# A megakernel of attention and a mixed feed-forward block: the gate's product, the last residuals and the order of PSUM banks

## The reference

```python
x = x + attn(_layernorm(x), Wqkv, bqkv, Wo, bo)
x = x + ffn(_layernorm(x), gate_w, up_w, down_w, fc1_w, fc2_w, expert_w, ln_gamma, ln_beta)

# attn: qkv = x @ Wqkv + bqkv (D = 256); softmax(q k^T / 16) v; @ Wo + bo
# ffn:
logits = x @ gate_w                                   # 1024 -> 8
routing_weights, _ = top_k(logits, 2)
shared_out = relu(x @ up_w) ** 2 @ down_w             # 1024 -> 2048 -> 1024
moe_out = (x @ fc1_w) @ expert_w * sum(routing_weights)   # 1024 -> 512 -> 512
routed_out = moe_out @ fc2_w                          # 512 -> 1024
ffn = _layernorm(shared_out + routed_out) * ln_gamma + ln_beta
```

## Time and profile before

| | |
|---|---|
| median of three runs | 2235.44 us (2233.91 to 2235.86) |
| profiled execution, its own time | 2224.65 us |
| profiled execution, span (first to last instruction) | 2222.9 us |
| PE busy | 2194.1 us (99%), 14963 matmuls |
| DVE busy | 1481.5 us (67%) |
| ACT busy | 623.9 us (28%) |
| POOL busy | 631.7 us (28%) |
| granted TensorE clock | 0.999 of full speed |
| HBM traffic | 202 GB/s over the span |

### The profile page before, as it was taken

How to read it: one execution, slowest core, us unless ns; L and a number is a source line. 1 busy time by engine, 2 the same in 40 slices (tenths; PEclk the granted TensorE clock), 3 DMA queues, 4 the chain that set the end, 5 groups by cost and what they waited for, 6 DMA issues and landing times.

```text
span 2222.9 us, 36661 instructions
## 1 busy us (share of the span) xinstructions
PE 2194.1 (99%) x14963; PEld 1418.4 (64%) x14963; DVE 1481.5 (67%) x1846; ACT 623.9 (28%) x966; POOL 631.7 (28%) x526
## 2 busy tenths in 40 slices
PE   7999999999999999999999999999999999999998
PEld 6756556666665444685487478468558748846853
DVE  7767387788985899776666377366556637737624
ACT  4334244345322664232022012112202201211210
POOL 2322000000002779255145024214404403421411
PEclk9999999999999999999999999999999999999999
DMA  9898288999897888879877987986997798798775
GB/s 234 196 215 220 58 183 234 243 242 224 185 212 203 291 310 287 283 238 286 272 215 225 278 273 220 287 283 205 279 273 231 225 284 259 220 295 264 205 231 167
DMA packets 527705, 530.05 MB, mean 238 GB/s; under 512 B 334896, under 2 KB 355504, under 8 KB 527536
## 3 DMA queue, kind: packets, MB, share of 16 engines
q1 hardware_dynamic: 513760, 495.70, 78.7%
q10 hardware_dynamic: 12912, 28.85, 4.2%
q0 software_dynamic: 864, 3.15, 0.4%
HBM read 375.03 MB, written 73.41 MB: 202 GB/s over the span
## 4 chain that ended last, share of the span: by engine, by line
PE 93%; DVE 4%; issue 2%; POOL 1%; DMA 0%; ACT 0%; DVEq 0%; ACTq 0%; POOLq 0%; SPq 0%
PE psum L99 62%; PE psum L2326 27%; PE psum L2270 4%; POOL arena L329 1%; DVE arena L2017 0%; PE psum L2235 0%; DVE arena L990 0%; DVE arena L540 0%; DVE c_ystats L2011 0%; PE psum L2236 0%; DMA arena<-arena 0%; DVE b_mx L1007 0%; DVE arena L2027 0%; DVE a_stats L496 0%; DVE arena L2029 0%
## 5 line engine op out<-in xcount | busy, mean ns | idle before, releaser
L99 PE MATMUL psum<-arena 128*128 128x256 f16 (+1 forms) x10920 | 1461.2, 297 | 5.0 <-ACT arena L879 1.5
L99 PEld LDWEIGHTS psum<-arena 128*128 128x128 f16 x10920 | 1067.5, 98 | 395.9 <-issue 4.5
L2326 PE MATMUL psum<-arena 128*128 128x512 f16 x2856 | 617.7, 379 | 0.0
L2326 PEld LDWEIGHTS psum<-arena 128*128 128x128 f16 x2856 | 279.4, 98 | 335.5
L1672 POOL TENSOR_TENSOR arena<-arena 128x256 f32<-128x256 f32 x70 | 98.4, 1405 | 350.6 <-ACT arena L1833 350.6
L879 ACT ACTIVATE arena<-psum,b_nb,consts 128x512 f32<-128x512 f32 x128 | 97.9, 774 | 196.3 <-DVE b_nb L1011 196.3
L1659 POOL TENSOR_TENSOR arena<-arena 128x256 f32<-128x256 f32 x68 | 50.5, 743 | 333.5 <-DVE arena L2113 277.0
L1990 DVE TENSOR_TENSOR arena<-arena 128x1536 f16<-128x1536 f32 (+1 forms) x28 | 60.6, 2165 | 121.5 <-ACT arena L1732 121.1
L1810 ACT ACTIVATE arena<-arena 128x768 f16<-128x768 f32 x68 | 57.3, 843 | 270.6 <-DVE arena L2113 229.5
L1814 ACT ACTIVATE arena<-arena 128x1024 f16<-128x1024 f32 x68 | 71.9, 1057 | 210.7 <-POOL arena L1665 207.7
L2073 DVE TENSOR_TENSOR arena<-arena 128x768 f16<-128x768 f32 x68 | 89.1, 1310 | 41.1 <-ACT arena L1810 40.9
(11 more groups left out here) (179 smaller groups left out, 1847.8 us busy)
## 6 DMA issues: line engine op xcount, KB each, us to landing
arena<-ws_out SPq DMA_DIRECT2D x238, 512.0 KB, 4.8
arena<-ws_in SPq DMA_DIRECT2D x210, 512.0 KB, 4.6
arena<-in_attn_x SPq DMA_DIRECT2D x64, 512.0 KB, 4.9
arena<-x SPq DMA_DIRECT2D x64, 512.0 KB, 6.6
arena<-ws_in SPq DMA_DIRECT2D x70, 256.0 KB, 4.8
x<-arena SPq DMA_DIRECT2D x32, 512.0 KB, 3.5
out<-arena SPq DMA_DIRECT2D x31, 512.0 KB, 6.2
ws_in<-arena SPq DMA_DIRECT2D x30, 512.0 KB, 4.5
```

The lines of the kernel that those rows point to most:

```text
L99: last = nc.tensor.matmul(out, lhs(a, c), rhs(b, c), start=(c == 0 and n == 0), stop=(c == chunks - 1 and n == len(PRODUCTS) - 1))
L2326: mm = nc.tensor.matmul(product_banks(m)[:, u, :], rS[c][:, a, LEFT[m], u * P:(u + 1) * P], w2[slot_of(i, d_slot(i, m, q))][:, cc, b, :], ...
```

## The change

Four edits, with what goes with them:

1. The gate of blocks 1 to 7. G11 is common to both halves of the block. It now has two rows of its own in `pG` (`G_ROWS` is 6: two with Y1 and G22, two with G21, two with G11), and DVE adds it to both halves with one more instruction, which waits for the first. A gate has 32 chunk products of two matmuls instead of 40. Block 0's gate keeps its four rows on PE; on DVE its sum of high and low is now two instructions of two tiles each. `g16` and `lg` grow from four to six rows, and for space the raw gate weights are scaled in place.
2. In the last block POOL adds beta to the residual of all four tiles, and DVE takes L2024 for all four.
3. In merged blocks (2 to 7) the statistics of the half of a tile that the outstanding product does not touch are taken before the wait for that product (`early_stats`).
4. The eight banks of the routed products begin with bank 7 instead of bank 6. The waits are changed to match: a routed product waits for one more of ACT's copies in block 0 and for the counts of its bank in block 1, the gate for one `rt_added` instead of two, and step p = 0 of the next block for five instead of six.

```diff
-BANKS_F, BANKS_U, BANK_G, BANKS_R = (7, 0), (0, 1, 2, 3), 7, (6, 7, 0, 1, 2, 3, 4, 5)
+BANKS_F, BANKS_U, BANK_G, BANKS_R = (7, 0), (0, 1, 2, 3), 7, (7, 0, 1, 2, 3, 4, 5, 6)
...
-    gs = sb("gs", [P, KC, NE], F32)
+    gs = graw
...
+    G_ROWS = 3 * HT
+    gate_rows = lambda i: TILES if first_turn(i) else G_ROWS
...
-            for q in range(R_EARLY, TILES):
+            for q in range(TILES):
                 pool.wait_ge(xres_in[q % 2], 16 * (2 * i + q // 2 + 1))
                 pool.tensor_tensor(xres[q % 2], xres[q % 2], beta, ALU.add).then_inc(xres_summed, 1)
...
-            nc.scalar.activation(g16[:], pG, ACT.Copy).then_inc(g_free, 1)
+            n = gate_rows(i)
+            nc.scalar.activation(g16[:, 0:n], pG[:, 0:n], ACT.Copy).then_inc(g_free, 1)
...
-        steps.done(dve.tensor_tensor(lg[:], g16[:, :, 0:NE], g16[:, :, NE:2 * NE], ALU.add))
+        if first_turn(i):
+            for t in range(0, TILES, HT):
+                at = slice(t, t + HT)
+                steps.done(dve.tensor_tensor(lg[:, at], g16[:, at, 0:NE], g16[:, at, NE:2 * NE], ALU.add))
+        else:
+            steps.link(dve.tensor_tensor(lg[:], g16[:, :, 0:NE], g16[:, :, NE:2 * NE], ALU.add))
+            halves = lg[:, 0:TILES].rearrange("p (h u) e -> p h u e", h=2)
+            shared = lg[:, TILES:].rearrange("p (h u) e -> p h u e", h=1).to_broadcast([P, 2, HT, NE])
+            steps.done(dve.tensor_tensor(halves, halves, shared, ALU.add))
...
-                if last and q >= R_EARLY:
+                if last:
-                    dve.wait_ge(xres_summed, q - R_EARLY + 1)
+                    dve.wait_ge(xres_summed, q + 1)
...
+        def early_stats(i, last, q, h):
+            steps.at(start + i * PER_BLOCK + ROUTE + (-q if last else NORM_S * TILES) + OUT * q)
+            steps.done(dve.bn_stats(ystats[:, h, :], acc[:, r_order(i)[q], h * BANK:(h + 1) * BANK]))
...
                     for u in range(HT):
-                        n = HT * (m - M3) + u
+                        n, h = HT * (m - M3) + u, m - M3
+                        early_stats(i, last, n, 1 - h)
...
-                        routed(i, last, range(n, n + 1))
+                        routed(i, last, range(n, n + 1), halves=(h,), done=1)
...
-                pe.wait_ge(rt_added, R_TILES * i + 2)
+                pe.wait_ge(rt_added, R_TILES * i + 1)
...
-            parts = ((Y1, 0), (G11, 0), (G22, KH)) if t < HT else ((G11, 0), (G21, KH))
+            parts = (((Y1, 0), (G22, KH)), ((G21, KH),), ((G11, 0),))[kind]
...
-        for t in range(TILES):
+        for t in range(gate_rows(i)):
...
-                    pe.wait_ge(acc_copied, n + 1)
+                    pe.wait_ge(acc_copied, min(n + 2, R_TILES))
-                    pe.wait_ge(d_added, added_by(i) + (3, 5, 6, 7)[n // 2])
+                    pe.wait_ge(d_added, added_by(i) + (5, 6, 7, 3)[BANKS_R[n] // HALVES])
...
-                        pe.wait_ge(rt_added, R_TILES * i + (6, R_TILES)[p])
+                        pe.wait_ge(rt_added, R_TILES * i + (5, R_TILES)[p])
```

More of the change, by code:

```diff
@@ L1195, in mixture @@
     beta = place(AT["c_beta"], [H], F32)
-    g16 = sb("g16", [P, TILES, 2 * NE], F32)
-    lg = sb("lg", [P, TILES, NE], F32)
+    G_ROWS = 3 * HT
+    g16 = sb("g16", [P, G_ROWS, 2 * NE], F32)
+    lg = sb("lg", [P, G_ROWS, NE], F32)
     top = sb("top", [P, TILES, 8], F32)
@@ L1217, in mixture @@
     u_half = lambda p, q: u_bank(p, q).rearrange("p (c n) -> p c n", c=2)
-    pG = bank(BANK_G)[:, 0:TILES * 2 * NE].rearrange("p (t e) -> p t e", t=TILES)
+    pG = bank(BANK_G)[:, 0:G_ROWS * 2 * NE].rearrange("p (t e) -> p t e", t=G_ROWS)
+    gate_rows = lambda i: TILES if first_turn(i) else G_ROWS
     e_in, c2_in, gb_in = sem("e_in"), sem("c2_in"), sem("gb_in")
@@ L1888, in act_program @@
         turns(body)
-    NORM, NORM_S, ROUTE, OUT = 4, 3, 1 + TILES + 1, 5
+    NORM, NORM_S, ROUTE, OUT = 4, 3, 2 + TILES + 1, 5
     BEFORE = 2
@@ L1995, in routing, with routed @@
             assert steps.n == ROUTE
-        def routed(i, last, tiles=range(TILES)):
-            steps.at(start + i * PER_BLOCK + ROUTE + (-max(tiles[0] - R_EARLY, 0) if last else NORM_S * TILES) + OUT * tiles[0])
+        def routed(i, last, tiles=range(TILES), halves=(), done=0):
+            steps.at(start + i * PER_BLOCK + ROUTE + (-tiles[0] if last else NORM_S * TILES) + OUT * tiles[0] + done)
             for q in tiles:
                 t = r_order(i)[q]
-                for h in range(HALVES):
+                for h in halves or range(HALVES):
                     n = HALVES * q + h
@@ L2029, in routed @@
                 dve.tensor_tensor(row, row, xres[q % 2], ALU.add).then_inc(out_ready, 1)
-            assert steps.n == OUT * len(tiles) - len([q for q in tiles if last and q >= R_EARLY])
+            assert steps.n == OUT * len(tiles) - done - (len(tiles) if last else 0)
+        def early_stats(i, last, q, h):
+            steps.at(start + i * PER_BLOCK + ROUTE + (-q if last else NORM_S * TILES) + OUT * q)
+            steps.done(dve.bn_stats(ystats[:, h, :], acc[:, r_order(i)[q], h * BANK:(h + 1) * BANK]))
         def first_body():
@@ L2222, in pe_gate, with rows_of @@
             else:
-                pe.wait_ge(rt_added, R_TILES * i + 2)
-        def rows_of(t):
+                pe.wait_ge(rt_added, R_TILES * i + 1)
+        def rows_of(n):
             if first_turn(i):
-                return [(k, lambda a, k=k: hT[:, a, k, t * P:(t + 1) * P]) for k in range(KC)]
-            cols = slice(t % HT * P, (t % HT + 1) * P)
-            parts = ((Y1, 0), (G11, 0), (G22, KH)) if t < HT else ((G11, 0), (G21, KH))
+                return [(k, lambda a, k=k: hT[:, a, k, n * P:(n + 1) * P]) for k in range(KC)]
+            kind, cols = n // HT, slice(n % HT * P, (n % HT + 1) * P)
+            parts = (((Y1, 0), (G22, KH)), ((G21, KH),), ((G11, 0),))[kind]
             return [(k + at, lambda a, s=s, k=k: hS[:, a, s, k, cols]) for s, at in parts for k in range(KH)]
-        for t in range(TILES):
+        for t in range(gate_rows(i)):
             rows = rows_of(t)
```

## The result

| | before | after |
|---|---|---|
| median of the timed runs | 2233.91 us (5 runs, 2231.48 to 2235.86) | 2221.38 us (5 runs, 2220.73 to 2222.34) |
| profiled execution, its own time | 2224.65 us | 2220.89 us |
| its span | 2222.9 us | 2219.1 us |
| start of the third attention stretch to the end | 1908.06 us | 1904.19 us |

The ratio of the timed runs is 0.995 [0.9936, 0.9963], 12.5 us less. The forecast was 2232.0 (2229.3 to 2235.3), so it was wrong. For a profiled execution the forecast was 2221.3, and 2220.89 was measured: the two traces differ by 3.76 us, the sum said 3.4. Both chains have a piece of 390.46 us of PE that starts at 314.84 before and at 314.91 after. From there on PE never waits for a transfer in either trace, and no instruction that the edits change runs ahead of it (the gate weights are scaled at 630 us).

A forecast was written before the change was run, and what follows sets the result against it. PE was taken to bound the kernel, busy 2194.1 of 2222.9 us. Gates 2.41, join 0.30 and tail 0.68 sum to 3.4 us, from 2235.44 to a median of 2232.0 us, range 2229.3 to 2235.3.

The forecast's parts named there:

- the first one of the sum: Outside the profiled span: the 10.8 us by which the unprofiled median exceeds the profiled execution, carried over unchanged to 2235.44 us.
- Gates: Gates of blocks 2 to 7: 16 matmuls fewer each at 25.1 ns, 0.40 us per gate, 2.41 us less.
- Rival F: Gates: removed weight loads cost their full 95 ns, 9.1 us there, 10.1 us in all, 2225.3 us; chance 0.01.
- The covers: Gate joins: 8 us of cover in block 3 before DVE's adds delay PE, so DVE's extra add costs nothing.
- D: Gates: the 0.4 us given back at each join by a wait that now just fits; 1 us gain, 2234.4; chance 0.10.
- E: Route: DVE's second add costs seven blocks 1.5 us each, 10.5 us less the 3.4; slower, 2242.5 us; chance 0.05.
- Join: Blocks 0 and 1: p = 0 could start 1.33 us earlier, but ACT's gate copy holds p = 1; gain 0.30 us.
- rival C: Join: p = 1 not held by the copy, whole 1.33 us won; 5.0 us in all, 2230.5; chance 0.13.
- rival B: Tail: POOL does not meet L2024, gain 1.22 us there, 3.9 us in all, 2231.5; chance 0.24.
- Tail: End of last block: one statistic less behind the last add, POOL colliding with tile 2's L2024; gain 0.68 us.
- The forecast's fear for that case: Tail: if POOL comes before L2017, tile 2 has both of its operations held up and the gain is near 0.
- faster by over 0.2%: Whole kernel: measured faster than no change by over 0.2%, 4.5 us, i.e. under 2230.97 us; chance 0.27.

The follow-up runs named there:

- e12: The kernel before, unchanged, one of five more profiled executions: 2225.11 us, 1907.5 us from the third stretch to the end.
- e14: The changed kernel, unchanged, twelve more runs beside the kernel before: median 2223.91 us, ratio 0.9982.
- e5: The kernel before with 14 of the 16 raw `up` loads cut to 64 of 1024 columns: median 2226.38 us, runs in two clusters.
- e6: The changed kernel with the same small raw loads as e5: median 2221.37 us.
- e10: e6 with ACT's gate copy ahead of block 0's last square root and the last two tiles' residuals loaded early: median 2219.55 us.
- quiet runs: Runs of kernels with 14 of the 16 raw `up` loads cut to 64 of 1024 columns; e5, the kernel before so cut, has median 2226.38 us.
- e9: The kernel before with the bank order (edit 4) alone and e5's small raw loads: median 2224.37 us, on another chip than e5.
- e11: The kernel before, unchanged, one of five more profiled executions: 2231.57 us, PE waiting 6.2 us for transposed input.
- e13: The kernel before, unchanged, one of five more profiled executions: 2231.57 us, PE waiting 4.3 us for transposed input.
- e3: The kernel before with the gate's edit (edit 1) alone, whole raw loads, twelve runs: median 2229.48 us, ratio 1.0002 to the kernel before.
- e4: The kernel before with the bank order and its waits (edit 4) alone, whole raw loads, twelve runs: median 2225.37 us, ratio 0.9998.
- y1: The changed kernel with e10's two further edits and whole raw loads: median 2221.66 us, ratio 0.9966 to the kernel before.
- e2: The changed kernel, unchanged, twelve runs again: median 2223.39 us, ratio 0.9978 to the kernel before; its traced execution took 2228.46 us.
- e1: The kernel before, unchanged, twelve runs against itself: median 2229.32 us, ratio 1.0012.
- e8: The kernel before with edits 2 and 3 (the tail) alone and e5's small raw loads: median 2225.00 us.
- y2: y1 with the sixteen raw loads spread over blocks 2 to 6 instead of 3 to 6: median 2226.28 us, ratio 0.9981 to the kernel before.

## Why the prediction was wrong

1. **The step that failed** is the first one of the sum: the 10.8 us between the profiled execution and the median were carried over unchanged, as if they were an overhead around the span. They were not outside it. The three runs shown were long ones of a kernel whose runs lie between 2223.63 and 2241.90, half of 130 of them above 2229 us; the profiled execution was a short one. The five timed runs before were all long (2231.48 and more), the five after all short (2222.34 and less), while of 24 further runs of the changed kernel nine were above 2225.5. Of the 12.5 us, 3.3 are shown as the edits' work in a usual execution (1907.5 to 1904.2 from the third stretch to the end), and up to 2 more come from the clock at the join (point 4). The rest is variation ahead of the third stretch, where the edits change no instruction. Whether they still change how often a run is long is open (below). The sign was visible in the rows that the forecast used: it said that three runs lay within 1.95 us and took that for the scatter, when the profiled execution itself, 10.8 us away with a span only 1.75 us shorter than its time, was a fourth run of the same kernel.
2. **Gates**: right. 2.42 us in the traces, 2.4 in the lower clusters, 2.41 forecast. Rival F is out: weight loads of 95 ns would have given 9.1. The covers held: no wait of PE at the joins of blocks 2 to 7 (rivals D and E are out).
3. **Join**: right in size and mechanism in a usual execution, 0.33 us (e12 and e14) and, with the same reckoning, 0.29 (e5 and e6), against 0.30 forecast. p = 1 is held by ACT's copy, and e10, which moves the copy, has no hold. So rival C is out; its price of 5.0 us also counted rival B's gain in the tail. The hold is 0.45 us and not the 1.0 forecast, and p = 0 gained about 0.8 us and not 1.33: the rows showed an unusual execution, whose wait for L2008 was 0.94 us, against 0.2 to 0.7 in the ten other traces of the old order. The 0.88 us between the first two traces are 0.3 of the edit and 0.5 of that execution, in which DVE's L2017 took 2.18 us beside POOL's sum and put everything behind it later.
4. **The clock at the join**: a term that the forecast lacks. With the old order some executions lose 1.7 us more through the clock behind the wait: two of eleven traces show it, and 16 of 33 quiet runs lie in the upper clusters, against none of 24 with the new order (e6, e9, e10). Together with point 3 this is why edit 4, priced at 0.30, takes 2 us off the quiet median (2226.38 to 2224.37, on two chips).
5. **Tail**: near in size (0.57 against 0.68), but by another way than forecast, which is partly luck: another instruction was held. The load for the last tile landed 3.39 us after its issue (2202.71 to 2206.10) instead of the 4.00 read from the earlier trace rows, and POOL caught tile 2's subtraction, not its L2036. (The 1.15 us that the forecast took from POOL's end to DVE's is 1.09 in its own rows, 2208.62 to 2209.71; that moves nothing.) The forecast's fear for that case, both operations held and no gain, did not come true: only one was held, for POOL's sum was over at 2208.45, 1.3 us before L2036 began.
6. **Chances**: "faster by over 0.2%" had 0.27. The two comparisons of the changed kernel with many runs give 0.9978 and 0.9982, on that line, their intervals reaching across it; the first ten runs gave 0.995, far beyond it. The forecast took the scatter for 1 us, and it is 10 us and more.

**Still open.** Runs of the kernel before above 2234 us (34 of 130, granted clock 0.996 to 0.998 over the span where it is on record) were caught in no trace, so that they too lose their time in attention's input is inferred from e11 and e13, not shown. Nor is it settled why kernels with the new bank order have fewer of the longest runs. The kernel before lies more than 8 us above its lowest run in 52 of 130 runs, e3 (the gate alone) in 4 of 12; the changed kernel in 3 of 29, e4 (the bank order alone) in none of 12. y1 had no run above 2227.04, while 19 of the 29 runs of the kernel before beside it were above, so that the medians are 10 us apart there and only 3 to 4 in the comparisons of e2 and e14. The 1.7 us at the join are too small for that. An effect of the edits on the long runs is thus a rival to chance that nothing here rules out; e3 and e4, with twelve runs each, do not decide it.

## What to carry to other kernels

Where the profiled execution and the timed median differ by more than the edits are worth, the first thing to explain is that difference: subtract the span from the time of the same run, and what is left over is variation inside the program. Compare two traces from an anchor behind the part that varies; here the stretch from 315 us to the end was 1907.4 to 1907.6 us in five executions and 1908.1 in the first trace, while whole runs varied by 18. One trace can itself be unusual, as the first was at the join, so take a second before pricing a wait of tenths of a microsecond. A short wait of PE behind light work is worth more than its length if the clock falls with it (here 1.67 us behind 0.4), and taking a wait away only gives what the next holder allows, so read that engine's order first.

## What the runs showed of the hardware

- A wait of 0.4 or 0.5 us of TensorE behind 2 us of matmuls of 16 and 8 columns was followed in two of eleven traces (e1, e8) by some 3 us at the 1.2 GHz level (granted clock 0.50 from 925 to 926 us), a cost of 1.67 us. The other nine had waits of 0.2 to 0.9 us and no fall. With no wait behind the gate no trace showed a fall (after, e2, e4, e6, e9, e10, e14, y1, y2). The Trainium skill, page "TensorE: Matmul & The Clock Gate", section "What's actually happening", has a clock whose two levels are 1.2 GHz for an idle engine and 2.4 GHz for a busy one. The levels agree with the granted clock of 0.50 and 1.00; that so short a wait is followed by a fall in a part of the executions is this case's measurement.
- The landing of the same transposing transfer varied from run to run. Counted from the end of its issue it was 17.3 us in e2, 17.4 in e11 and 14.6 in e13, and SyncE's pair of issues took 10.04 us in e2 where it took 3.43 in the first trace after. In the first traces of both kernels PE did not wait for it at all. With 14 of the 16 raw loads made small, the kernel before scattered over 2.5 us instead of 14.
- DVE's 128x1024 operation with two SBUF operands, 1.23 to 1.28 us alone, took 3.25 when POOL's sum ran beside it, and ended 1.1 us after POOL's end, before (2208.62 to 2209.71) and after (2208.45 to 2209.53) alike.
